# Experts' rows added into X in DRAM by the scatter's own transfers, and a feed-forward opened in another order

## The chip, the cores and the metric

One core of a Trainium2 chip runs the whole kernel in one launch. The metric is the device time of an execution in microseconds (us); less is better. The kernel before was run three times.

## What is computed

Two layers over 16 sequences of 128 tokens of 256 numbers (2048 tokens), each a gated cross-attention and a gated feed-forward, added to x. Cut to what the change touches:

```python
x = x + tanh(g_xattn[0]) * mlstm(layernorm(x), ctx, ctx, ...)
x = x + tanh(g_ffn[0])   * ffn0(layernorm(x), ...)     # 8 experts, 2 per token, and 2 shared ones
x = x + tanh(g_xattn[1]) * attention(layernorm(x), ctx, mask, ...)   # 16 heads of 16
x = x + tanh(g_ffn[1])   * ffn1(layernorm(x), ...)     # 16 experts in 4 groups, 4 per token, and a shared one

# ffn0
logits = xf @ router_w.T + expert_bias
rw, sel = top_k(logits, 2); rw = softmax(rw)
combine = einsum('tk,tke->te', rw, one_hot(sel, 8))
out = sum over e of combine[:, e] * (silu(xf @ w1[e].T) * (xf @ w3[e].T)) @ w2[e].T
out = out + the same for the two shared experts, without weights
```

## The kernel before

X, the 2048 rows of x, stays on the chip as 128 partitions x 16 sequences x 256, in four chunks of four sequences (`CH` = 4, `NCH` = 4). The work goes through five stages in one program; each engine has its own list of instructions, written out by hand, and semaphores join them.

The first attention (`front`, `cell`) and the shared experts of the first feed-forward (`shared_feed_forward`) come first. While the shared experts run, each token's normalised row is scattered twice into `xg_dram`, sorted by expert, with its destination and its weight behind it. `routed_tiles` then takes 39 tiles (`NT`) of 128 such rows. For a tile i, SyncE loads its rows into `t_x` (L2121), TensorE turns them (L2144), makes gate (L2153 to L2155) and up (L2162), turns the hidden rows (L2169) and makes the down product (L2180); ScalarE and VectorE copy between them; VectorE multiplies by the row's weight (L2252); and GpSimd scatters the 128 result rows into `y_dram` in DRAM (`send`, L2134). Each token has two places there, one for each of its experts, and the blank rows of partly filled tiles have places of their own. `y`, `dest` and `t_x` have two buffers each. With the last `t_x` load SyncE issues the seven loads of `later` (L2124): the weights, context and masks of the second attention.

`attention_feed_forward` holds the second attention and the second feed-forward. It opens with the projections of keys and values of chunks 0 and 1, which need no x. When all scatters have landed, SyncE loads both places of every token into `picked` (L728), 8 transfers for 4 chunks. VectorE adds chunk 0 to X (`add_first`, L1247), GpSimd adds chunks 1 to 3 (L787) in 12 instructions. Then come, chunk by chunk, the layer norm: `statistics2` (VectorE, L1256, L1259), `deviation2` (ScalarE's square root, L1075), `scale2` (VectorE), `normalise2` (both); TensorE turns the rows (`project` of kind "x", L846), and makes the queries from them (L858). A softmax step s (16 of them, one per sequence) is: scores (TensorE, L873), `soft` (VectorE, twice, L1286 and L1289), `centre` (GpSimd, L814), `exps` (ScalarE, L1092 and L1096), turning (TensorE, L885), `keep_turned` (ScalarE for three quarters, VectorE for the last, L1295), `values` (TensorE, L897), and the output added to X by GpSimd (L822).

The feed-forward runs in steps u, 12 (`U`) per chunk: `gate_up(u)` and `down(u)` (L981) on TensorE, `silu` (L1136) and `keep_hhi` (L1147) on ScalarE, `hidden` on VectorE. Beside the steps of a chunk the next chunk is prepared; a function `step(u, c)` says at which step which piece comes: statistics, deviation, normalise, turning (`turn_xn`, L920), the copies of the turned rows (`keep_hi`, `keep_lo`), router (L931), the route steps on VectorE (`route_logits` to `route_weights`), `turn_comb` and `keep_comb`, after which SyncE stores the combine weights and loads them as `cb`. The third block of weights is split by ScalarE in two halves (`last_block_hi`, L1142) and by VectorE in three thirds.

The order of the first steps of VectorE before, word for word:

```python
for n in range(2):
    keep((0, "v", n))
add_first()
statistics2(0)
scale2(0)
normalise2(0)
keep((0, "x", 1))
for n in range(2):
    keep((1, "v", n))
statistics2(1)
scale2(1)
normalise2(1)
```

## Time and profile before

| | us |
|---|---|
| median of 3 runs | 883.3 |
| lowest, highest | 883.18, 890.21 |
| the profiled execution | 890.36 |
| its span | 888.2 |
| expert tiles, first to last scatter's issue | 276.9 to 483.4 |
| loads of `picked` start | 485.77 |
| TensorE busy, whole span | 783.9 |

The span is what the profiler saw of the instructions; the execution's own time is a little longer. The three runs lie on two levels, and the profiled execution on the upper. Times of instructions are counted from the span's start. A row of the view in order of time gives start, length, engine, line, operation, output<-input and number of instructions, and in brackets the engine's idle time before it and what ended it. PE is TensorE's products, PEld its weight loads, DVE VectorE, ACT ScalarE, POOL GpSimd, SPq SyncE's transfers.

### The profile page before, as it was taken

What the parts mean: (1) busy time and instruction counts of PE and PEld (TensorE: products, weight loads), DVE (VectorE), ACT (ScalarE), POOL (GpSimd) and SP (SyncE); (2) the same over time, 40 slices, a digit from 0 to 9 for tenths busy, and PEclk for the clock granted to TensorE, in tenths of its full rate; (3) what the DMA queues carried; (4) which work ended last, traced back from release to release, by engine and by line L of the source; (5) the groups of instructions that cost most, each with busy time, mean ns of one, the idle gap of its engine ahead of it and who ended that gap; (6) DMA issues with size and microseconds to landing.
All of it is one profiled execution on the core that took longest, in us unless ns stands there. A gap on an engine that the chain in (4) does not pass through costs nothing.

```text
span 888.2 us, 14817 instructions
## 1 busy us (share of the span) xinstructions
PE 783.9 (88%) x5188; PEld 609.4 (69%) x5188; DVE 512.2 (58%) x1188; ACT 395.6 (45%) x806; POOL 220.4 (25%) x220
## 2 busy tenths in 40 slices
PE   4556399999999999999999778996788999999997
PEld 3345277788887777777776445664567888888886
DVE  4478865565454444333342678879755675756644
ACT  5468545234342222222222378787645335253322
POOL 0179110026602111111113448675210000000000
PEclk9788889999999999999999879999888999999999
DMA  8357651013241111111133800202004005050130
GB/s 296 122 187 288 229 203 59 1 54 120 90 154 42 49 49 49 52 50 48 49 90 114 290 0 13 75 11 73 1 1 97 1 1 120 1 120 1 37 84 25
DMA packets 33591, 74.32 MB, mean 84 GB/s; under 512 B 4400, under 2 KB 20400, under 8 KB 31760
## 3 DMA queue, kind: packets, MB, share of 16 engines
q1 hardware_dynamic: 30112, 64.03, 23.0%
q0 software_dynamic: 3408, 9.34, 2.9%
q8 instruction: 44, 0.72, 0.3%
q14 instruction: 27, 0.22, 0.1%
HBM read 61.73 MB, written 16.78 MB: 88 GB/s over the span
## 4 chain that ended last, share of the span: by engine, by line
PE 61%; DVE 11%; ACT 5%; issue 4%; DVEq 3%; DMA 1%; POOL 1%; POOLq 1%; SPq 0%; ACTq 0%
PE t_y_ps L2180 8%; PE t_up L2162 8%; PE f_y L1743 4%; PE a_turned L981 4%; PE a_score L959 3%; PE a_score L961 3%; PE a_score L960 3%; PE a_turned L885 2%; PE t_gate L2153 2%; PE t_gate L2154 2%; PE t_gate L2155 2%; PE t_h_turned L2169 2%; PE a_proj L858 2%; PE a_out_ps L981 1%; PE f_gate L1724 1%
## 5 line engine op out<-in xcount | busy, mean ns | idle before, releaser
L2212 ACT CAST t_xT_hi<-t_x_turned 128x256 fp32r<-128x256 f32 x39 | 14.5, 372 | 150.3 <-PE t_x_turned L2144 150.3
L2134 POOL DMA_INDIRECT outputs<-t_y,t_dest x39 | 37.4, 959 | 177.4 <-DVEq L2253 174.8
L2180 PEld LDWEIGHTS t_y_ps<-W,t_hidT 128*128 128x128 f32 x312 | 59.2, 190 | 25.2 <-issue 19.2
L2180 PE MATMUL t_y_ps<-W,t_hidT 128*128 x312 | 73.8, 379 | 0.8 <-ACT t_hidT L2222 0.8
L2162 PE MATMUL t_up<-W,t_xT 128*128 x156 | 73.4, 593 | 0.0
L1147 ACT CAST a_hhi<-a_hid 128x512 fp32r<-128x512 f32 x48 | 29.8, 620 | 76.9 <-DVEq L1441 76.9
L1136 ACT ACTIVATE a_act_g<-a_score 128x512 f32<-128x512 f32 x48 | 28.7, 597 | 59.0 <-PE a_score L961 58.8
L1443 DVE TENSOR_TENSOR a_hlo<-a_hid,a_hhi 128x512 fp32r<-128x512 f32 x48 | 33.2, 693 | 35.1 <-ACT a_hhi L1147 35.1
L2241 DVE TENSOR_TENSOR t_hid<-t_act_g,t_up 128x512 f32<-128x512 f32 x39 | 26.8, 688 | 38.5 <-ACT t_act_g L2217 34.2
L1096 ACT ACTIVATE a_pr<-a_sc,a_nmx 128x128 f32<-128x128 f32 x128 | 40.8, 391 | 13.4 <-DVE a_nmx L1289 13.4
L814 POOL TENSOR_TENSOR a_sc<-a_sc,a_nmx 128x512 f32<-128x512 f32 x32 | 33.2, 1039 | 51.8 <-DVE a_nmx L1289 51.8
L2232 DVE COPY t_xT<-t_x_turned 128x256 f32<-128x256 f32 x39 | 16.6, 425 | 47.0 <-ACT t_xT_hi L2212 46.9
L885 PE MATMUL a_turned<-cst,a_pr 128*128 128x128 f32 x256 | 41.0, 297 | 1.9 <-ACT a_prT L1102 1.9
L1286 DVE TENSOR_TENSOR a_sc<-a_score,a_pen 128x1024 f32<-128x1024 f32 x32 | 38.9, 1217 | 5.8 <-PE a_score L873 4.5
L443 ACT ACTIVATE W<-W,AT 128x128 f32<-128x128 f32 x128 | 38.2, 390 | 7.1 <-POOL W L359 7.1
L2252 DVE TENSOR_SCALAR t_y<-t_y_ps,t_dest 128x256 f32<-128x256 f32 x39 | 18.9, 483 | 38.8 <-PE t_y_ps L2180 38.8
L1289 DVE TENSOR_REDUCE a_nmx<-a_sc 128x8 f32<-128x1024 f32 x32 | 39.0, 1220 | 2.9
L897 PE MATMUL a_out_ps<-a_prT,a_v 128*32 128x128 f32 x512 | 25.8, 295 | 16.5 <-issue 10.7
L2162 PEld LDWEIGHTS t_up<-W,t_xT 128*128 128x128 f32 x156 | 26.6, 190 | 18.6 <-issue 18.6
L2153 PE MATMUL t_gate<-whi,t_xT_hi 128*128 x78 | 37.9, 486 | 1.3 <-DVE t_xT_lo L2233 1.3
L885 PEld LDWEIGHTS a_turned<-cst,a_pr 128*128 128x128 f32 x256 | 30.0, 151 | 11.7 <-issue 8.7
L1651 POOL DMA_INDIRECT slot_tokens<-W,slots x32 | 34.0, 1064 | 15.1 <-issue 15.1
...
## 6 DMA issues: line engine op xcount, KB each, us to landing
...
t_x<-slot_tokens SPq DMA_DIRECT2D x39, 129.0 KB, 2.0
...
```

Of the source, the lines that this page charges most:

```text
L443: last = act.activation(dmat[i % 2][:, q, k, r], expo[i % 2][:, q, k, r], ACT.Exp, bias=AT[:, at:at + 1], scale=-1.0)
L885: last = pe.transpose(turned[n % 2][:, i * 128:(i + 1) * 128], pr[s % 2][:, g, i], cst[:, C_ID:C_ID + 128])
L981: last = pe.matmul(y_bank[use % 3][:, (j % 2) * D:(j % 2 + 1) * D], h[q][:, j * 128:(j + 1) * 128], w_[:, down_cols(ht)], start=first, sto ...
L1096: last = act.activation(pr[s % 2][:, g, i], sc[s % 2][:, g, i], ACT.Exp, bias=nmx[s % 2][:, g, i:i + 1])
L1286: dve.tensor_tensor(part, score[:, half * 1024:(half + 1) * 1024].rearrange("p (h t) -> p h t", h=8), pen[c % 2][:, j:j + 1].broadcast_to( ...
L1289: dve.tensor_reduce(nmx[s % 2][:, 2 * half:2 * half + 2].rearrange("p r i -> p (r i)"), part, AX.X, ALU.max, negate=True).then_inc(max_rea ...
L1651: pool.indirect_dma_start(xg_dram, bass.IndirectOffsetOnAxis(ap=slots[:, k, s:s + 1], axis=0), XN[:, s, :], None).then_inc(done, 16)
L1743: last = pe.matmul(y_bank[use % 3][:, (j % 2) * D:(j % 2 + 1) * D], h_[q][:, j * 128:(j + 1) * 128], w_[:, down_cols(ht)], start=first, st ...
L2134: pool.indirect_dma_start(y_dram, bass.IndirectOffsetOnAxis(ap=dest[p][:, 0:1].bitcast(U32), axis=0), y[p][:], None).then_inc(y_stored[p], 16)
L2153: pe.matmul(gate[p][:], xT_hi[p][:, k], W_hi[:, ds(e, 1), cols], start=(k == 0), stop=False)
L2162: last = pe.matmul(up[p][:], xT[p][:, k], W[:, ds(e, 1), at:at + HID], start=(k == 0), stop=(k == KT - 1))
L2180: last = pe.matmul(y_ps[p][:, 0:D], hidT[p][:, h], W[:, ds(e, 1), at:at + D], start=(h == 0), stop=(h == HT - 1))
```

## The change

It has four parts.

1. The sum in DRAM. `y_dram` goes; `sum_dram` has one row per token and 128 rows that are written by blank rows only (set to zeros early, so that they hold numbers). SyncE stores X into it, chunk by chunk, as soon as a chunk is complete: chunks 0 and 1 behind the load of expert 7's weights, chunk 2 between the loads of expert 1's weights, chunk 3 behind the second `t_x` load. GpSimd's scatters have a `compute_op` that adds to the row at the destination; the first waits for all stores, and each waits for the one before. At the attention's opening X is loaded from there in four transfers. `picked`, `add_first` and GpSimd's adds go.
2. The order at the attention's opening, on VectorE and ScalarE: statistics and scales of chunks 2 and 3 ahead of the first softmax; chunk 1's statistics ahead of the copy of chunk 0's second turned half; one small activation loads the square root's table while ScalarE waits for the scatters.
3. The end of the attention: VectorE's copy of the last turned probabilities comes ahead of `route_logits` and of `route_second`, which goes behind the first hidden product. `last_block_hi(0)` moves from step 2 to step 1.
4. The steady feed-forward: for chunks 2 and 3 turning and all that follows it come one step later; statistics, deviation and normalising stay.

```diff
@@ cell, SyncE @@
             sp.dma_start(xg_dram.rearrange("(p i) d -> p (i d)", p=128),
                          blank_rows.rearrange("(p i) d -> p (i d)", p=128)).then_inc(slots_blank, 16)
+            sp.dma_start(sum_dram[T:T + 128, :], blank_rows[0:128, 0:D]).then_inc(sums_blank, 16)
@@ attention_feed_forward @@
-        by_dve = [(0, "v", 0), (0, "v", 1), (0, "x", 1), (1, "v", 0), (1, "v", 1)]
+        by_dve = [(0, "v", 0), (0, "v", 1), (1, "v", 0), (0, "x", 1), (1, "v", 1)]
...
         def step(u, c):
-            return u - ((c - 1) * U + (1 if c == 1 else 0))
+            k = u - ((c - 1) * U + (1 if c == 1 else 0))
+            return k if c == 1 or k < 2 else (k - 1 if k > 2 else None)
+
+        def normalised(u, c):
+            return u - ((c - 1) * U + (1 if c == 1 else 0)) == 2
@@ SyncE @@
-            rows = y_dram[0:2 * T, :].rearrange("(k s p) d -> p k s d", k=2, s=B)
             for c in range(NCH):
                 part = slice(c * CH, (c + 1) * CH)
-                for k in range(2):
-                    sp.dma_start(picked[:, k, part, :], rows[:, k, part, :]).then_inc(picked_loaded[c], 16)
+                sp.dma_start(X[:, part, :], sums[:, part, :]).then_inc(x_loaded[c], 16)
@@ GpSimd @@
-            pool.wait_ge(first_added, 1)
-            for c in range(1, NCH):
-                pool.wait_ge(picked_loaded[c], 32)
-                for half in range(2):
-                    at = slice(c * CH + 2 * half, c * CH + 2 * half + 2)
-                    for k in range(2):
-                        last = pool.tensor_tensor(X[:, at, :], X[:, at, :], picked[:, k, at, :], ALU.add)
...
@@ ScalarE @@
+            act.activation(largest[:, 0, 0:1], cst[:, C_EPS:C_EPS + 1], ACT.Sqrt)
+
             for p in range(2):
                 act.wait_ge(y_stored[p], 16 * ((NT + 1 - p) // 2))
-            for n in range(2):
-                keep((1, "k", n))
+            keep((1, "k", 0))
             deviation2(0)
             normalise2(0)
+            keep((1, "k", 1))
             keep((0, "x", 0))
             deviation2(1)
-            for n in range(2):
-                keep((0, "q", n))
             normalise2(1)
+            keep((0, "q", 0))
+            deviation2(2)
+            keep((0, "q", 1))
+            deviation2(3)
...
-                if 2 <= u < 4:
-                    last_block_hi(u - 2)
+                if u in (1, 3):
+                    last_block_hi(u // 2)
@@ VectorE @@
             def statistics2(c):
-                wait(dve, picked_added, c)
+                dve.wait_ge(x_loaded[c], 16)
...
-            add_first()
             statistics2(0)
             scale2(0)
             normalise2(0)
+            keep((1, "v", 0))
+            statistics2(1)
             keep((0, "x", 1))
-            for n in range(2):
-                keep((1, "v", n))
-            statistics2(1)
+            keep((1, "v", 1))
             scale2(1)
             normalise2(1)
+            for c in (2, 3):
+                statistics2(c)
+            for c in (2, 3):
+                scale2(c)
...
                 keep(early)
+                if s == B:
+                    route_groups(0)
+                if past:
+                    keep_turned(s - 1, 3)
                 if s == B - 1:
                     route_logits(0)
-                elif s == B:
-                    route_groups(0)
-                    route_second(0)
-                if past:
-                    keep_turned(s - 1, 3)
...
                 elif s == B:
                     hidden(0)
+                    route_second(0)
                     route_pick(0)
@@ shared_feed_forward, SyncE @@
+            def store(c):
+                sp.wait_ge(y_free, 2 * c + 2)
+                sp.dma_start(sums[:, c * CH:(c + 1) * CH, :], X[:, c * CH:(c + 1) * CH, :]).then_inc(x_stored[c], 16)
...
@@ routed_tiles, SyncE and GpSimd @@
                 sp.dma_start(x[p][:], xg_dram[ds(i * 128, 128), :]).then_inc(x_loaded[p], 16)
+                if i == 1:
+                    sp.wait_ge(y_free, 2 * NCH)
+                    sp.dma_start(sums[:, (NCH - 1) * CH:, :], X[:, (NCH - 1) * CH:, :]).then_inc(x_stored[NCH - 1], 16)
...
             def send(i, p, nth):
                 pool.wait_ge(y_ready, i + 1)
+                wait(pool, y_stored[1 - p], 16 * ((i + 1) // 2))
                 pool.sem_inc(sent, 1)
-                pool.indirect_dma_start(y_dram, bass.IndirectOffsetOnAxis(ap=dest[p][:, 0:1].bitcast(U32), axis=0), y[p][:],
-                                        None).then_inc(y_stored[p], 16)
+                pool.indirect_dma_start(sum_dram, bass.IndirectOffsetOnAxis(ap=dest[p][:, 0:1].bitcast(U32), axis=0), y[p][:],
+                                        None, compute_op=ALU.add).then_inc(y_stored[p], 16)
+            pool.wait_ge(sums_blank, 16)
+            for c in range(NCH):
+                pool.wait_ge(x_stored[c], 16)
```

How the instructions stand in a row, at the three places that matter. SyncE's list at the start of the tiles, before (W: expert weights, t_x: a tile's rows):

```order
L1633 DMA W<-in_w_dram 128x2560
L1635 DMA W<-in_w_dram 128x512 [waits f_hlo_ready]
L2116 UNCONDITIONAL_BRANCH
L2121 DMA t_x<-slot_tokens 128x258 [waits f_h_used]
L2121 DMA t_x<-slot_tokens 128x258
L2121 DMA t_x<-slot_tokens 128x258 [waits t_dest_ready,t_xt_ready] x37
```

and after the change:

```order
L1619 DMA W<-in_w_dram 128x2560
L1603 DMA sums<-X 128x4x256 [waits f_y_free]
L1622 DMA W<-in_w_dram 128x512 [waits f_hlo_ready]
L2105 UNCONDITIONAL_BRANCH
L2110 DMA t_x<-slot_tokens 128x258 [waits f_h_used]
L2110 DMA t_x<-slot_tokens 128x258
L2113 DMA sums<-X 128x4x256 [waits f_y_free]
L2110 DMA t_x<-slot_tokens 128x258 [waits t_dest_ready,t_xt_ready] x37
```

The first of the stores shown is chunk 2's, ahead of the last part of expert 1's weights; the second is chunk 3's, and it stands between the second and the third `t_x` load and waits for the last sum of X.

VectorE at the attention's opening before, behind chunk 0's normalised rows and up to the first softmax (a_XNT: turned rows, a_v: values, a_stats: statistics, a_pr: normalised rows, a_sc: scores with the mask):

```order
L1226 COPY a_XNT<-a_turned 128x2x256 [waits a_proj_ready]
L1238 SCALAR_TENSOR_TENSOR a_v<-a_score,g_tanh,a_bvt 128x16x16 [waits a_proj_ready]
L1238 SCALAR_TENSOR_TENSOR a_v<-a_score,g_tanh,a_bvt 128x16x16
L1238 SCALAR_TENSOR_TENSOR a_v<-a_score,g_tanh,a_bvt 128x16x16 [waits a_proj_ready]
L1238 SCALAR_TENSOR_TENSOR a_v<-a_score,g_tanh,a_bvt 128x16x16
L1256 BN_STATS a_stats<-X 128x6 [waits a_picked_added]
L1256 BN_STATS a_stats<-X 128x6 x3
L1259 BN_AGGR a_mean_var<-a_stats 128x2 x4
L1265 RECIPROCAL a_rstd<-a_std 128x4 [waits a_std2_ready]
L1267 SCALAR_TENSOR_TENSOR a_shift<-a_mean_var,a_rstd 128x4
L1275 TENSOR_SCALAR a_pr<-X,a_mean_var,a_rstd 128x256 x2
L1286 TENSOR_TENSOR a_sc<-a_score,a_pen 128x1024 [waits a_pen_ready,a_score_ready]
```

and after:

```order
L1230 SCALAR_TENSOR_TENSOR a_v<-a_score,g_tanh,a_bvt 128x16x16 [waits a_proj_ready]
L1230 SCALAR_TENSOR_TENSOR a_v<-a_score,g_tanh,a_bvt 128x16x16
L1239 BN_STATS a_stats<-X 128x6 [waits a_x_loaded1]
L1239 BN_STATS a_stats<-X 128x6 x3
L1242 BN_AGGR a_mean_var<-a_stats 128x2 x4
L1218 COPY a_XNT<-a_turned 128x2x256 [waits a_proj_ready]
L1230 SCALAR_TENSOR_TENSOR a_v<-a_score,g_tanh,a_bvt 128x16x16 [waits a_proj_ready]
L1230 SCALAR_TENSOR_TENSOR a_v<-a_score,g_tanh,a_bvt 128x16x16
L1248 RECIPROCAL a_rstd<-a_std 128x4 [waits a_std2_ready]
L1250 SCALAR_TENSOR_TENSOR a_shift<-a_mean_var,a_rstd 128x4
L1258 TENSOR_SCALAR a_pr<-X,a_mean_var,a_rstd 128x256 x2
L1239 BN_STATS a_stats<-X 128x6 [waits a_x_loaded2]
```

Chunk 1's statistics and a copy of values moved ahead of the copy into `a_XNT`, and where the softmax stood the statistics of chunk 2 begin; those of chunk 3 and both scales follow before the softmax.

ScalarE there before, from chunk 0's square roots on (a_std: square roots, a_kbd: keys, a_qT: queries):

```order
L1075 ACT_TABLE_LOAD
L1075 ACTIVATE a_std<-a_mean_var,cst 128x4 [waits a_var2_ready]
L1084 ACTIVATE a_pr<-X,a_shift,a_rstd 128x256 [waits a_shift2_ready]
L1084 ACTIVATE a_pr<-X,a_shift,a_rstd 128x256
L1059 COPY a_XNT<-a_turned 128x2x256 [waits a_proj_ready]
L1075 ACTIVATE a_std<-a_mean_var,cst 128x4 [waits a_var2_ready]
L1063 ACTIVATE a_qT<-a_out_ps,a_bq 128x512 [waits a_proj_ready]
L1063 ACTIVATE a_qT<-a_proj,a_bq 128x512 [waits a_proj_ready]
L1084 ACTIVATE a_pr<-X,a_shift,a_rstd 128x256 [waits a_shift2_ready]
L1084 ACTIVATE a_pr<-X,a_shift,a_rstd 128x256
L1059 COPY a_XNT<-a_turned 128x2x256 [waits a_proj_ready] x2
```

and after:

```order
L1066 ACTIVATE a_std<-a_mean_var,cst 128x4 [waits a_var2_ready]
L1075 ACTIVATE a_pr<-X,a_shift,a_rstd 128x256 [waits a_shift2_ready]
L1075 ACTIVATE a_pr<-X,a_shift,a_rstd 128x256
L1059 ACTIVATE a_kbd<-a_score,a_bkm,cst 128x512 [waits a_proj_ready]
L1059 ACTIVATE a_kbd<-a_score,a_bkm,cst 128x512
L1050 COPY a_XNT<-a_turned 128x2x256 [waits a_proj_ready]
L1066 ACTIVATE a_std<-a_mean_var,cst 128x4 [waits a_var2_ready]
L1075 ACTIVATE a_pr<-X,a_shift,a_rstd 128x256 [waits a_shift2_ready]
L1075 ACTIVATE a_pr<-X,a_shift,a_rstd 128x256
L1054 ACTIVATE a_qT<-a_out_ps,a_bq 128x512 [waits a_proj_ready]
L1066 ACTIVATE a_std<-a_mean_var,cst 128x4 [waits a_var2_ready]
L1054 ACTIVATE a_qT<-a_proj,a_bq 128x512 [waits a_proj_ready]
```

The table load is gone from here (it stands ahead of the wait for the scatters now), a copy of keys went behind the first normalised rows, chunk 1's rows went ahead of the queries, and the root of chunk 2 stands between the two query copies.

## Rows read from the trace of the kernel before

**Rows 1.** Busy time by stretch (us; PE, PEld, DVE, ACT, POOL, PEclk, DMA, GB/s).

```profile
300.00:350.00 50.00, 50.00 (x218) 36.34 (x217) 19.88 (x56) 13.68 (x29) 8.63 (x9) 1.00 0.17 50
500.00:550.00 50.00, 38.19 (x301) 22.28 (x301) 39.02 (x71) 34.70 (x79) 33.67 (x35) 0.85 0.14 54
650.00:700.00 50.00, 44.12 (x269) 35.98 (x269) 31.31 (x94) 25.26 (x42) 2.50 (x3) 0.90 0.20 44
```

**Rows 2.** Instructions in order of time, the last tiles, POOL and DVE.

```profile
452.62 0.96 POOL L2134 DMA_INDIRECT outputs<-t_y,t_dest  x1 [4.53 <-DVEq L2253]
458.11 0.96 POOL L2134 DMA_INDIRECT outputs<-t_y,t_dest  x1 [4.54 <-DVEq L2253]
...
471.69 0.17 DVE L2245 COPY t_dest<-t_next_dest 128x2 int32<-128x2 int32 x1 [3.42 <-DMA outputs<-t_y,t_dest]
...
479.86 0.96 POOL L2134 DMA_INDIRECT outputs<-t_y,t_dest  x1 [4.27 <-DVEq L2253]
```

**Rows 3.** The tensor of results: all its scatters, then the one at 463.60 alone.

```profile
L2134 POOL DMA_INDIRECT outputs<-t_y,t_dest x39: 954/958/967, 276.9 to 483.4; - x39
...
DMA to landing us min/median/max: 2.4/2.4/10.8
...
L2134 POOL DMA_INDIRECT outputs<-t_y,t_dest x1: 958/958/958, 463.6 to 463.6; - x1
...
DMA to landing us min/median/max: 8.1/8.1/8.1
```

**Rows 4.** The page's transfers: KB each, median us from issue to landing.

```profile
t_x<-slot_tokens SPq DMA_DIRECT2D x39, 129.0 KB, 2.0
```

**Rows 5.** Instructions in order of time, the opening of the second attention.

```profile
491.06 2.52 DVE L1247 TENSOR_TENSOR X<-X,a_picked 128x1024 f32<-128x1024 f32 x2 [1.54 <-DMA a_picked<-outputs]
...
491.88 3.62 PE L851 MATMUL a_score<-a_w,a_keyT 128*128 128x256 f32 x16
...
493.68 1.40 DVE L1256 BATCH_NORM_STATS2 a_stats<-X 128x6 f32<-128x256 f32 x4
...
506.25 9.24 POOL L787 TENSOR_TENSOR X<-X,a_picked 128x512 f32<-128x512 f32 x7 [0.15 <-issue]
...
506.82 0.30 ACT L1075 ACTIVATE a_std<-a_mean_var,cst 128x4 f32<-128x4 f32 x1 [7.16 <-DVEq L1260]
...
510.21 1.21 DVE L1286 TENSOR_TENSOR a_sc<-a_score,a_pen 128x1024 f32<-128x1024 f32 x1
...
515.10 1.39 DVE L1256 BATCH_NORM_STATS2 a_stats<-X 128x6 f32<-128x256 f32 x4
...
519.11 1.23 DVE L1286 TENSOR_TENSOR a_sc<-a_score,a_pen 128x1024 f32<-128x1024 f32 x1 [0.19 <-issue]
...
522.39 1.28 ACT L1075 ACT_TABLE_LOAD   x1
...
530.47 1.22 DVE L1286 TENSOR_TENSOR a_sc<-a_score,a_pen 128x1024 f32<-128x1024 f32 x1 [1.94 <-PE a_score L873]
...
537.04 1.21 DVE L1286 TENSOR_TENSOR a_sc<-a_score,a_pen 128x1024 f32<-128x1024 f32 x1
...
544.04 1.22 DVE L1286 TENSOR_TENSOR a_sc<-a_score,a_pen 128x1024 f32<-128x1024 f32 x1
```

**Rows 6.** The output's last store, of 512 KB, alone on the queues.

```profile
L764 SPq DMA_DIRECT2D out_dram<-X x1: 377/377/377, 884.8 to 884.8; - x1
...
DMA to landing us min/median/max: 2.9/2.9/2.9
```

**Rows 7.** Instructions in order of time, the start of the tiles.

```profile
266.24 1.65 DVE L2067 SCALAR_TENSOR_TENSOR X<-f_y,g_tanh,X 128x256 f32<-128x256 f32 x4
...
271.22 0.38 PE L2144 MATMUL t_x_turned<-cst,t_x 128*128 128x128 f32 x2
```

**Rows 8.** Instructions in order of time, the opening of the second feed-forward.

```profile
661.20 0.43 PE L897 MATMUL a_out_ps<-a_prT,a_v 128*32 128x128 f32 x8 [1.63 <-DVE a_prT L1295]
...
674.76 1.48 ACT L1142 CAST a_block2hi<-a_raw 128x1536 fp32r<-128x1536 f32 x1
...
681.23 0.38 PE L981 MATMUL a_turned<-a_block0hi,a_hhi 128*128 128x256 f32 x1 [1.87 <-ACT a_hhi L1147]
```

**Rows 9.** Who waited for whom, 684 to 888 us: total, times, longest.

```profile
PE a_proj L920 <- DVE a_xn L1328: 1.8, 3, 0.7
```

65 lines of the change are left out of this document (25 added, 40 removed).

## The prediction

> **What bounds the kernel now.** I read the busy times by stretch first, then who waited for whom, and only then single instructions in order of time. In the expert tiles (300 to 350 us) TensorE has no gap at all, at the full granted clock, while VectorE, ScalarE and GpSimd have room. In 500 to 550 us it is busy for 38.19 of 50 us at a mean granted clock of 0.85: that is the opening of the second attention. In 650 to 700 us it is busy for 44.12, the opening of the second feed-forward [rows 1]. What the change does to work beside the tiles is worth nothing by itself; its worth has to be found at the two openings.
>
> The last expert's scatter is issued at 483.36 (483.4 in the view of its tile) and lands 2.4 us later, at 485.8 [rows 3], and then the eight loads of `picked` start. From there on [rows 5]: VectorE adds chunk 0 at 491.06 (2.52 us for both adds), the statistics begin at 493.68, GpSimd adds chunks 1 to 3 until 506.25 + 9.24 = 515.49. ScalarE's root for chunk 1, which needs those sums, begins at 506.82 and stands in its queue ahead of the copies of the queries, without which there are no scores; the first softmax starts at 510.21. After it VectorE has the statistics of chunks 2 and 3 (from 515.10) ahead of the next softmax at 519.11, and ScalarE loads another table at 522.39. The third softmax begins at 530.47; then a step takes 7.00 us (537.04 to 544.04).
>
> **Part 1: the sums made by the transfers.** What goes: 4 of 8 loads of 512 KB, VectorE's two adds and GpSimd's twelve. What comes: each scatter adds to rows in DRAM, and each waits until the one before has landed. How long such a scatter takes stands in no row. From below it can be as short as a plain one, 2.4 us to landing, of which 0.96 is GpSimd writing the descriptors [rows 3]. From above I take a plain one and a read of its own, as long as the load of the same rows into `t_x`, 2.0 us [rows 4]: 4.4; further out lies the 8.1 us that a plain one took from 463.60 on, beside the seven loads for the attention [rows 3]. I take the middle of the first two, 3.4. The Trainium skill (DMA: Bandwidth & Descriptors, Rules for kernel authors) says that an accumulating transfer reads its destination and writes it later, so that the next one has to wait for its semaphore. The change does that; the trace of before has no accumulating transfer to compare. The same page (Latency and other measured facts) gives about 0.8 us as the least round trip to DRAM; a plain 2.4 and that would make an estimate of 3.2.
>
> A tile takes 5.49 us (scatters at 452.62 and 458.11 [rows 2]), so at 3.4 us each scatter has landed before the next result is ready, and the added wait costs nothing. Nothing else stands behind it on GpSimd until the tiles end, and VectorE waits only for the scatter two tiles back. Two places have no such room. Beside the seven loads a scatter took 8.1 us and VectorE stood 3.42 us for it, at 471.69 [rows 2]; a longer one there holds TensorE up by at most what it adds, 1.0; I take 0.5, between 0 and 2.0. At the end scatter 37 is issued at 479.86 [rows 2] and lands at 483.3, and 38, issued at 483.4 as before, lands at 486.8 instead of 485.8: 1.0 (0 if it is a plain one; 2.9 at 4.4 us each, since 38 is then also issued 0.9 later).
>
> The rows of X have to be in DRAM first. The stores of chunks 0 to 2 fall beside the shared experts, and ahead of nothing on SyncE that is soon wanted. The store of chunk 3 stands ahead of the third `t_x` load, whose rows are turned at 271.22 now. That load would come after the last sum of X (266.24 + 1.65 = 267.89 [rows 7]), behind 512 KB in the same queue. A store of this size took 2.9 us alone [rows 6]; some 1.5 of that I take as data. So the load lands near 268.4 + 2.0 + 1.5 = 271.9 against 271.22: 0.7, between 0 and 3.
>
> **Part 2: the attention's opening.** I go on from the new landing at 486.8. X's chunk 0 is one transfer of 512 KB instead of two: between 2.9 us (the store alone) and the 5.3 us of the first pair (485.8 to 491.06), I take 3.8: 490.6. Statistics (1.40 and their grouping), the root (0.30, its table loaded before), scale and the normalised rows take some 4.1: 494.7. TensorE still projects values of chunk 1 until 491.88 + 3.62 = 495.5 and turns the rows by some 496.7. VectorE's copy of them now stands behind a copy of values and chunk 1's statistics: 498.0. The queries are as much work as those values, 3.6: 501.7. ScalarE copies the first half by 501.1, then waits until 502.0 for chunk 2's statistics on VectorE, takes the root and copies the second by 503.1. The first scores run to 504.3, chunk 3's root and the two scales end at 505.1, and the first softmax starts at 505.1: 5.1 earlier than 510.21, with the later scatter already in it.
>
> From the first softmax to the third it is 530.47 - 510.21 = 20.26 us now, against 14.0 for two steady steps. What goes of the difference: VectorE's statistics, 4.0 (515.10 to 519.11); two table loads of ScalarE (1.28 each, one at 522.39); and GpSimd's adds until 515.49, which hold up its own part of the first softmax [rows 5]. They overlap, and the floor is 14.0. I take 14.9, which gives 5.4 more. From the third softmax on both run at 7.00 a step and nothing is given back. Sum of this part: -10.5. I count nothing for the granted clock, though shorter gaps may raise its 0.85 here.
>
> **Part 3: the feed-forward's opening.** TensorE waits 1.63 us at 661.20 for VectorE's copy of the last turned probabilities, which stands behind two route steps [rows 8]. Now it stands behind one, and TensorE gets 1.1 back. But VectorE idles those 1.1 until the turning is done, with all its route steps still to do, so its product for step 1 comes 1 us later and TensorE loses the gain there. The first half of the third weight block (1.48 us of ScalarE at 674.76) moves a step forward, where ScalarE has idle time; it stood ahead of the activation whose product TensorE waits for, 1.87 us at 681.23 [rows 8]. With VectorE's 1.0 against it 0.4 is left: -0.4.
>
> Later turning: for chunks 2 and 3 the rows are turned one step after they are normalised, where TensorE now waits 0.6 each (1.8 in three waits [rows 9]; that of chunk 1 stays): -1.2. All route steps of the two chunks come one step later too; their combine weights are then made at the same distance from their use as chunk 1's now, and the waits from 684 us on show none for `cb`.
>
> **The sum:** -10.5 + 0.5 + 0.7 - 0.4 - 1.2 = -10.9. The profiled execution took 890.36 us (span 888.2, the rest lies around it), so 879.5 for its like. The median of the runs is 883.3, 7.1 below the profiled one: two runs are near 883 and one is at 890.21. I put the difference on the median: 872.4, given as 872.5.
>
> **Rivals.** A, the opening keeps much of its length: the chain through statistics, turning and queries is serial, the statistics of chunks 2 and 3 now stand ahead of the first softmax, and the two first steps still carry extra copies and projections, so VectorE and ScalarE become the bound. For it speaks that ScalarE's second query copy waits for chunk 2's statistics; against it, that VectorE idles there anyway. Then only the 5.1 to the first softmax come, less 0.5 and 0.7 and with part 3: -5.5, 878. B, the transfers become the bound of the tiles: an adding scatter with twice the 0.96 us of descriptors, a read of 2.0, the 1.4 that is left of a plain one and 0.7 for the add takes 6.0, and with half a us from landing to the next issue it paces a tile at 6.5 instead of 5.49. Over 38 tiles +38, less 10 at the openings: 911. It decides from about 5.0 us per scatter on; for it speaks only that a plain one took 8.1 in company. C, more comes: TensorE keeps its clock through the opening (the mean is 0.85 now) and the first two steps come near their floor: -16, 867. D, the last scatters pile up behind the seven loads: two of 8 us in a row delay VectorE and then the end of the tiles by 4 to 5: 877.
>
> **How the numbers follow.** Forecast 0.55, A 0.17, B 0.10, C 0.09, D 0.09. Faster by over 1% is below 874.5, and about 1% is what a measurement of this kernel can tell from no change. The forecast's own range is 868 to 877, of which some three quarters lie below (0.42); with C and a part of A and D (0.05) that is 0.56. Slower is B and a little for what I overlooked: 0.11. The rest, 0.33, is within 1%. The range takes in C below, and A, D and a median that falls on the upper of the two levels above: 866 to 884; B stays outside.
>
> **What would show it.** In the profile after: scatters of 3 to 4 us to landing and tiles still 5.49 apart; the third turning of `t_x` at most 3 us later; the first softmax 18 us after the last landing and the third 15 later; one table load fewer on either side of it; TensorE's wait at the last turned probabilities smaller by 1.1, and two of three waits for `a_xn` gone. A tile pace above 5.5, a scatter above 5 us, or a first softmax that is not earlier would make the forecast wrong.

## The result, and the profile after

| | before | changed |
|---|---|---|
| median, on the first chip | 885.12 us (9 runs, 881.27 to 890.21) | 879.03 us (9 runs, 875.92 to 881.86) |
| ratio | | 0.9929, 95% interval 0.9901 to 0.9956 |
| the profiled execution | 890.36 | 876.65 |
| its span, mean granted clock | 888.2, 0.952 | 874.8, 0.966 |

The change takes 6.1 us off the medians (0.7%), where 10.9 were forecast. The two profiled executions differ by 13.7, more than twice that, so the first thing to learn is which part of that difference belongs to the change and which to the draw of two executions. Two executions of the kernel before beside e5 to e8 took 1950 and 2992 us (the others 887 to 898) and are in none of the ratios there.

The busy times of the three stretches after:

```profile
300.00:350.00 50.00, 50.00 (x218) 36.37 (x218) 20.09 (x56) 13.65 (x29) 14.57 (x10) 1.00 0.30 49
500.00:550.00 50.00, 42.00 (x365) 24.54 (x365) 41.19 (x77) 38.40 (x90) 24.73 (x28) 0.93 0.15 59
650.00:700.00 50.00, 47.03 (x268) 40.58 (x267) 33.96 (x102) 22.85 (x33) 0.73 (x1) 0.97 0.21 44
```

The tiles have no gap on TensorE, as before. GpSimd is busy for 14.57 us there in place of 8.63, and the DMA share is 0.30 in place of 0.17: that is the adding, since in e10, the same kernel without it, they are 8.62 and 0.16. At both openings TensorE has smaller gaps and a higher clock than in [rows 1].

The page's row of the adding scatter (instructions, busy time and mean ns of one), and its tile's view of the 35 from 300 us on (busy ns of one, then us from issue to landing):

```profile
L2127 POOL DMA_INDIRECT sums<-t_y,t_dest x39 | 60.8, 1559 | 160.3 <-DVEq L2249 142.2
...
L2127 POOL DMA_INDIRECT sums<-t_y,t_dest x35: 1556/1557/1558, 299.3 to 488.4; - x35
...
DMA to landing us min/median/max: 3.7/3.9/9.6
```

It lands after 3.9 us in place of 2.4 and takes GpSimd 1.56 us in place of 0.96 [rows 3]. The forecast took 3.4 to landing. (Both views of the tile count the loads from it too: the 10.8 us in [rows 3] is a load of `picked`, and the longest landing of a scatter there is 8.1.)

The last tiles in order of time, GpSimd's and VectorE's rows, which answer to [rows 2]:

```profile
458.61 1.56 POOL L2127 DMA_INDIRECT sums<-t_y,t_dest  x1 [3.94 <-DVEq L2249]
464.10 1.56 POOL L2127 DMA_INDIRECT sums<-t_y,t_dest  x1 [3.94 <-DVEq L2249]
474.50 1.56 POOL L2127 DMA_INDIRECT sums<-t_y,t_dest  x1 [8.85 <-DMA sums<-t_y,t_dest]
479.01 1.56 POOL L2127 DMA_INDIRECT sums<-t_y,t_dest  x1 [2.95 <-DMA sums<-t_y,t_dest]
483.93 1.56 POOL L2127 DMA_INDIRECT sums<-t_y,t_dest  x1 [3.36 <-issue]
488.39 1.56 POOL L2127 DMA_INDIRECT sums<-t_y,t_dest  x1 [2.90 <-DMA sums<-t_y,t_dest]
...
473.77 0.17 DVE L2241 COPY t_dest<-t_next_dest 128x2 int32<-128x2 int32 x1 [5.01 <-DMA sums<-t_y,t_dest]
...
478.28 0.17 DVE L2241 COPY t_dest<-t_next_dest 128x2 int32<-128x2 int32 x1 [2.39 <-DMA sums<-t_y,t_dest]
...
482.88 0.17 DVE L2241 COPY t_dest<-t_next_dest 128x2 int32<-128x2 int32 x1 [1.84 <-DMA sums<-t_y,t_dest]
```

The pace of 5.49 us holds up to the scatter at 464.10. The next is released by a landing (`<-DMA sums`), not by VectorE, 10.4 us later, and then they follow at 4.5 to 4.9. VectorE, which may not overwrite `dest` before its scatter has landed, waits 5.01, 2.39 and 1.84 us where it waited 3.42 once.

The start of the tiles, as in [rows 7]:

```profile
267.18 0.38 PE L2140 MATMUL t_x_turned<-cst,t_x 128*128 128x128 f32 x2
271.65 0.44 PE L2140 MATMUL t_x_turned<-cst,t_x 128*128 128x128 f32 x2 [0.98 <-DMA t_x<-slot_tokens]
```

A wait of 0.98 us for the third load of `t_x`, where TensorE had none. In e5 and e13, two more executions of the same kernel, it is 0.78 and none.

The attention's opening after, which answers to [rows 5]:

```profile
495.92 1.41 DVE L1239 BATCH_NORM_STATS2 a_stats<-X 128x6 f32<-128x256 f32 x4 [4.39 <-DMA X<-sums]
...
504.26 1.40 DVE L1239 BATCH_NORM_STATS2 a_stats<-X 128x6 f32<-128x256 f32 x4
...
511.02 1.23 DVE L1269 TENSOR_TENSOR a_sc<-a_score,a_pen 128x1024 f32<-128x1024 f32 x1 [0.67 <-PE a_score L864]
...
515.96 1.22 DVE L1269 TENSOR_TENSOR a_sc<-a_score,a_pen 128x1024 f32<-128x1024 f32 x1
...
523.55 1.22 DVE L1269 TENSOR_TENSOR a_sc<-a_score,a_pen 128x1024 f32<-128x1024 f32 x1 [0.64 <-PE a_score L864]
...
488.66 1.28 ACT L1143 ACT_TABLE_LOAD   x1
...
492.18 2.03 SPq L729 DMA_DIRECT2D X<-sums  x4
```

X is asked for at 492.18 and its first chunk has landed at 495.92. VectorE then has the statistics of all four chunks ahead of the first softmax at 511.02. From there to the third (523.55) it takes 12.53 us in place of 20.26 (17.1 and 18.9 in e8 and e7, which have the opening of the kernel before), and ScalarE's table load for the roots stands at 488.66, where ScalarE had nothing to do.

Who waited for whom on TensorE at the end of the attention and in the feed-forward (total, times, longest):

```profile
PE a_turned L972 <- ACT a_hhi L1138: 3.5, 5, 1.7
PE a_proj L930 <- DVE a_comb L1394: 1.3, 1, 1.3
PE a_out_ps L972 <- ACT a_hhi L1138: 0.5, 1, 0.5
PE a_out_ps L888 <- DVE a_prT L1278: 0.4, 1, 0.4
```

The wait for the turned probabilities is 0.4 in place of 1.63, that for `a_xn` is gone, and one for the combine weights (1.3) is new.

### The profile page after: what moved, and what is told of

It reads as the page before. It is cut to its first block, busy times and chain, and to the rows that moved or that the text cites. A ratio compares the mean times of both kernels' runs of the same rounds, so it can differ in the third digit from the quotient of the medians.

```text
span 874.8 us, 14796 instructions
## 1 busy us (share of the span) xinstructions
PE 773.7 (88%) x5188; PEld 601.4 (69%) x5188; DVE 507.3 (58%) x1186; ACT 392.6 (45%) x805; POOL 228.9 (26%) x208
## 4 chain that ended last, share of the span: by engine, by line
PE 54%; DVE 15%; ACT 8%; issue 4%; DMA 4%; DVEq 4%; SPq 0%; ACTq 0%; POOLq 0%
PE t_y_ps L2176 7%; PE t_up L2158 7%; PE f_y L1730 4%; DMA sums<-t_y,t_dest 3%; PE a_turned L972 2%; PE a_turned L876 2%; ACT a_hhi L1138 2%; PE a_score L950 2%; PE a_score L952 2%; PE a_score L951 2%; PE a_proj L849 2%; DVE a_hlo L1426 2%; PE t_gate L2150 2%; PE t_gate L2151 2%; PE t_gate L2149 2%
## 5 line engine op out<-in xcount | busy, mean ns | idle before, releaser
L2127 POOL DMA_INDIRECT sums<-t_y,t_dest x39 | 60.8, 1559 | 160.3 <-DVEq L2249 142.2
L1087 ACT ACTIVATE a_pr<-a_sc,a_nmx 128x128 f32<-128x128 f32 x128 | 40.8, 391 | 13.2 <-DVE a_nmx L1272 12.5
L2248 DVE TENSOR_SCALAR t_y<-t_y_ps,t_dest 128x256 f32<-128x256 f32 x39 | 18.9, 484 | 37.1 <-PE t_y_ps L2176 37.1
L2158 PEld LDWEIGHTS t_up<-W,t_xT 128*128 128x128 f32 x156 | 26.6, 191 | 18.6 <-issue 18.6
L876 PE MATMUL a_turned<-cst,a_pr 128*128 128x128 f32 x256 | 38.2, 282 | 0.5 <-ACT a_prT L1093 0.5
L888 PE MATMUL a_out_ps<-a_prT,a_v 128*32 128x128 f32 x512 | 24.7, 286 | 15.2 <-issue 10.9
L1418 DVE TENSOR_TENSOR a_hid<-a_score,a_cb 128x512 f32<-128x512 f32 x32 | 22.1, 691 | 21.8 <-PE a_score L952 19.1
```

The source lines that it names most:

```text
L876: last = pe.transpose(turned[n % 2][:, i * 128:(i + 1) * 128], pr[s % 2][:, g, i], cst[:, C_ID:C_ID + 128])
L1087: last = act.activation(pr[s % 2][:, g, i], sc[s % 2][:, g, i], ACT.Exp, bias=nmx[s % 2][:, g, i:i + 1])
L2127: pool.indirect_dma_start(sum_dram, bass.IndirectOffsetOnAxis(ap=dest[p][:, 0:1].bitcast(U32), axis=0), y[p][:], None, compute_op=ALU.add) ...
L2158: last = pe.matmul(up[p][:], xT[p][:, k], W[:, ds(e, 1), at:at + HID], start=(k == 0), stop=(k == KT - 1))
```

## The measure for the experiments

The start of the tiles (the first turning of `t_x`) falls at 263.96 us in this profile and at 273.11 in another one of the same kernel. Most stretches behind it are steady to some tenths; F and D are not, as said below. So the experiments are read by seven stretches, each between two rows: A from the first turning of `t_x` to the first scatter; B from there to the last scatter; C to the first statistics of X; D to ScalarE's first exponents (L1087); E to its exponents of the third softmax; F to its last exponents; G to the last write of X. All are in us, in the traces of the kernel before, of that kernel with one wait added (e8) and with seven loads spread (e7), neither of which changed its time, and of the changed kernel in three executions.

| | before | e8 | e7 | changed | e5 | e13 |
|---|---|---|---|---|---|---|
| A | 12.17 | 12.17 | 12.16 | 13.49 | 13.28 | 12.57 |
| B | 206.51 | 206.55 | 206.52 | 210.94 | 211.11 | 210.17 |
| C | 10.32 | 10.59 | 10.53 | 7.53 | 7.67 | 7.53 |
| D | 19.76 | 19.12 | 19.61 | 18.06 | 17.15 | 17.18 |
| E | 20.74 | 19.33 | 18.56 | 13.61 | 13.61 | 13.61 |
| F | 117.41 | 116.70 | 114.74 | 113.58 | 117.81 | 113.85 |
| G | 231.57 | 229.77 | 229.63 | 228.57 | 229.00 | 230.01 |
| A to G | 618.48 | 614.23 | 611.75 | 605.78 | 609.63 | 604.92 |

The changed kernel averages 606.8 and the other three 614.8. In F the last step takes 5.0 us in the changed kernel's first trace and in e13, and 9.3 in e5, which is the same kernel. In e5 TensorE has no gap but half the clock from 642.4 to 651.7 us (granted 0.50; 1.00 in the same step of e13), as the stretch that holds this step shows (TensorE's busy time first, granted clock third from the end):

```profile
640.00:650.00 10.00, 10.00 (x80) 8.25 (x81) 5.28 (x5) 4.49 (x11) 3.04 (x4) 0.58 0.00 1
```

The kernel before was profiled in such an execution (9.6 us, clock 0.57 in the same stretch); e8 and e7 took 6.5. That is one reason why the two first profiles overstate the change.

## Experiments

Each ratio is to runs of the kernel before on the same chip, whose median there was 890.4 to 891.4 us; a median alone is not compared with one of the first chip.

**e1 and e12, the seven loads spread.** In SyncE's load function:

```diff
-                if isinstance(i, int) and i == NT - 1:
-                    for dst, src, loaded in later:
-                        sp.dma_start(dst, src).then_inc(loaded, 16)
+                for dst, src, loaded in later[i - (NT - 8):i - (NT - 8) + 1] if i >= NT - 8 else []:
+                    sp.dma_start(dst, src).then_inc(loaded, 16)
```

> The changed kernel with the seven loads for the attention (w, bqk, bv, keyT, pen) issued one behind each of the x loads of tiles 31 to 37, instead of all seven behind the load of tile 38. Theory (the last scatters pile up behind the seven loads, each adding scatter waiting for the one before it): the scatter of tile 34 lands about 4 us after its issue in place of 9.6, the VectorE waits of 5.01, 2.39 and 1.84 us in the last five tiles go or fall below 1 us, the first load of X is issued 4 to 6 us earlier than at 492.18 us, and the whole takes 4 to 5 us less than the changed kernel, about 874.5 us in the median. Rival 1 (the tiles are late by the adding scatters' own landing of 3.9 us and their serial wait, the loads are incidental): the first load of X moves by less than 1 us and the time stays at 879. Rival 2 (the load is 3.8 MB in any case and slows scatters wherever it stands): several tiles wait 1 to 2 us each, and the gain is below 2 us.

Measured: 879.57 us, ratio 0.9863 (0.9832 to 0.9893). GpSimd's rows of the last tiles:

```profile
475.25 1.56 POOL L2126 DMA_INDIRECT sums<-t_y,t_dest  x1 [3.94 <-DVEq L2248]
480.74 1.56 POOL L2126 DMA_INDIRECT sums<-t_y,t_dest  x1 [3.94 <-DVEq L2248]
486.35 1.56 POOL L2126 DMA_INDIRECT sums<-t_y,t_dest  x1 [4.04 <-issue]
490.76 1.56 POOL L2126 DMA_INDIRECT sums<-t_y,t_dest  x1 [2.86 <-DMA sums<-t_y,t_dest]
```

The pile-up is gone: B is 207.65, 3.3 less than in the changed kernel's trace, and rival 1 falls. What stays over 206.51 is 1.1, in the last two intervals (5.61 and 4.41 in place of 5.22 and 3.50); the last scatter waits for the one before. (The seven loads are 2.4 MB, by the sizes of the issues in the profile, not 3.8.) D was 15.56 too, 2.5 less. The two executions' rows show why (changed kernel first, then e1): the queries ran at half clock in the one (granted 0.50 from 502.7 to 506.5 us) and at full clock in the other. The next four products took 2.71 and 1.88.

```profile
502.74 3.75 PE L849 MATMUL a_out_ps<-a_XNT,a_w 128*128 128x512 f32 x4 [1.82 <-DVE a_XNT L1218]
```

```profile
505.16 1.96 PE L849 MATMUL a_out_ps<-a_XNT,a_w 128*128 128x512 f32 x4 [1.82 <-DVE a_XNT L1218]
```

To see whether this is worth its 4 to 5 us in the median, it was timed again beside the changed kernel itself.

> The changed kernel with the seven loads spread, once more, beside the changed kernel itself on the same chip. The stretches of the traces say 3.3 us from the first scatter to the last and 1.5 to 2.5 us in the queries' clock; one kernel's attention ends in 4.9 or 9.4 us for its last step from run to run, so single profiles and medians of few runs hide it. Theory (the pile-up is worth 4 to 5 us): the median is 3.5 to 5.5 us below that of the changed kernel in this call. Rival (what the last scatters give is taken back behind them, as the run with both repairs had it with 0.9901): less than 2 us below.

> The changed kernel as it is, beside the run before this one: 210.6 to 211.1 us from the first scatter to the last, a ratio to the kernel before of 0.991 to 0.994, and 3.5 to 5.5 us more than the kernel with the loads spread by the theory, under 2 us more by the rival.

Measured: 883.21 and 882.64 us, ratios 0.9906 (0.9877 to 0.9934) and 0.9921 (0.9890 to 0.9952). B was 207.80 against 210.17, so the tiles were again 2.4 shorter, but D was 17.18 in both: the full clock of the queries in e1 was a draw. The median with the loads spread is 0.6 us above that of the changed kernel beside it, not 4 to 5 below, and this theory of the size falls, though e1's ratio alone had agreed with it; by this pair it is under 2 as the rival had it. The rival's reason is not borne out either: from the first scatter to the last write of X e12 took 590.13 and e13 592.35, so nothing behind the tiles took the gain back. The starts of the tiles, 275.55 and 269.37, differ by more than what is looked for.

**e2, the store of chunk 3 behind the third load of `t_x`:**

```diff
-                if i == 1:
+                if i == 2:
```

> The changed kernel with the store of X's fourth chunk behind the load of x for tile 2 instead of ahead of it. Theory (the store on SP's queue holds up x(2)): TensorE's wait of 0.98 us for t_x at 271.65 us goes, the tiles start 0.5 to 1.1 us earlier, the whole is about 1 us shorter, which 5 rounds hardly tell from nothing; GpSimd's first scatter is not later, since tile 0's rows are ready only after the store has landed. Rival (hidden anyway: TensorE then waits for the copies of x_turned or for a later load): the milestone of tile 38 moves by less than 0.2 us. Rival 2: the store lands later and the first adding scatter waits for it, the first tiles lengthen by up to 1 us.

Measured: 885.15 us, 0.9908 (0.9881 to 0.9935). A was 12.28, that is 0.3 to 1.2 less than the changed kernel's three, and the wait of TensorE is gone; but e13 had no such wait either, so only the 12.28, met again in e11, speaks for the edit. The store does hold the load up; the price is small, and below what the median can tell.

**e3, the opening's order put back** (X still comes whole from DRAM):

```diff
+            keep((0, "x", 1))
-            keep((1, "v", 0))
-            statistics2(1)
-            keep((0, "x", 1))
-            keep((1, "v", 1))
+            for n in range(2):
+                keep((1, "v", n))
+            statistics2(1)
             scale2(1)
             normalise2(1)
-            for c in (2, 3):
-                statistics2(c)
...
-            act.activation(largest[:, 0, 0:1], cst[:, C_EPS:C_EPS + 1], ACT.Sqrt)
```

> The changed kernel with the order of the attention's opening put back as it was in the kernel before (statistics of chunks 2 and 3 and the deviations in step 0 and 1, keeps of keys and values ahead of the normalising, no early Sqrt), while X still comes whole from DRAM. Theory (the order carries the gain, as the forecast had it): from the first softmax to the third it takes again about 20 us in place of 12.5, or at least 17, and the whole is 5 to 8 us longer than the changed kernel. Rival (the gain comes from taking away the additions on GpSimd and VectorE and the second half of the loads alone, so that chunks 2 and 3 are there when step 0 wants them; the order is worth little): the third softmax moves by less than 2 us against the landing of X. Between them: 2 to 5 us, shared.

Measured: 888.36 us (12 runs), 0.9956 (0.9934 to 0.9979). VectorE's rows:

```profile
499.03 1.41 DVE L1238 BATCH_NORM_STATS2 a_stats<-X 128x6 f32<-128x256 f32 x4 [4.05 <-DMA X<-sums]
...
510.92 1.23 DVE L1268 TENSOR_TENSOR a_sc<-a_score,a_pen 128x1024 f32<-128x1024 f32 x1 [1.35 <-PE a_score L864]
...
515.82 1.40 DVE L1238 BATCH_NORM_STATS2 a_stats<-X 128x6 f32<-128x256 f32 x4
...
527.83 1.23 DVE L1268 TENSOR_TENSOR a_sc<-a_score,a_pen 128x1024 f32<-128x1024 f32 x1 [0.30 <-PE a_score L864]
```

With the old order the first softmax stands 11.89 us behind the first statistics, in place of 15.10, and the third 16.91 behind the first, in place of 12.53. The order moves work from between the softmaxes to ahead of them; at the third it is worth 1.2 us by these rows (28.80 against 27.63), 1.0 to 1.9 by D + E against the three executions. Without the order, D + E is 32.65, against 38.17 in e7, 38.45 in e8 and 40.50 in the kernel before: these 5.5 to 7.9 us come from the additions and the second half of the loads that are gone, which no run separates. So the rival holds in the traces. The median, 0.9956 against 0.9915 to 0.9929, says some 3 us for the order, with intervals that overlap; its profile had the last attention step in 9.6 us at a clock of 0.67 in 640 to 650, and whether the old order meets the half clock there more often stays open.

**e4, the router's steps and the halves of the third block put back:**

```diff
-                if s == B:
-                    route_groups(0)
-                if past:
-                    keep_turned(s - 1, 3)
                 if s == B - 1:
                     route_logits(0)
+                elif s == B:
+                    route_groups(0)
+                    route_second(0)
+                if past:
+                    keep_turned(s - 1, 3)
                 keep(late)
...
-                if u in (1, 3):
-                    last_block_hi(u // 2)
+                if 2 <= u < 4:
+                    last_block_hi(u - 2)
```

> The changed kernel with the router's steps (route_groups, route_second ahead of the copies again) and last_block_hi at u = 2 and 3 put back as in the kernel before. Theory (the forecast's -0.4 for this part): the waits of TensorE on a_prT (0.43 us) grows to about 1.6 us, that on a_comb (1.30 us) goes, hidden(0) to hidden(1) is shorter by about 1 us, and the whole stays within 1 us. Rival 1 (this part keeps the granted clock up: the kernel before ran at 0.57 in 640 to 650 us and at 0.66 in 680 to 690): the row at the end of the attention shows a stretch at half clock again and the whole is 3 to 4 us longer. Rival 2 (it costs: the a_comb wait is new and holds the second unit): the whole is 1 to 2 us shorter.

Measured: 882.64 us, 0.9915 (0.9885 to 0.9944). TensorE's waits:

```profile
PE a_out_ps L888 <- DVE a_prT L1278: 3.4, 2, 1.8
PE a_proj L911 <- DVE a_xn L1311: 0.8, 1, 0.8
```

The wait for `a_prT` is back, the one for `a_comb` gone. From the first silu to the last write of X it takes 222.58 us against 222.07, 222.50 and 222.08 of the changed kernel: 0.1 to 0.5, as forecast, and below what the medians can tell. Rival 1 does not hold in this trace, whose last attention step took 5.0 us again.

Its tiles, which the edit does not touch, show something else. GpSimd's rows:

```profile
468.02 1.56 POOL L2127 DMA_INDIRECT sums<-t_y,t_dest  x1 [3.93 <-DVEq L2249]
476.86 1.56 POOL L2127 DMA_INDIRECT sums<-t_y,t_dest  x1 [7.29 <-DMA sums<-t_y,t_dest]
481.19 1.56 POOL L2127 DMA_INDIRECT sums<-t_y,t_dest  x1 [2.78 <-DMA sums<-t_y,t_dest]
485.96 1.56 POOL L2127 DMA_INDIRECT sums<-t_y,t_dest  x1 [3.21 <-issue]
490.41 1.56 POOL L2127 DMA_INDIRECT sums<-t_y,t_dest  x1 [2.90 <-DMA sums<-t_y,t_dest]
```

The late scatter landed after 8.1 us and the next came 8.84 behind it, where the changed kernel's three executions have 10.0 to 11.0; B is 209.04, so 2.5 is lost and not 3.7 to 4.6.

**e5, the changed kernel again, and e6, the early stores moved.** In four profiles of kernels that differ from the changed one only behind this place (e1 to e4), TensorE stood 3 to 4 us in 200 to 220 us.

> The changed kernel as it is, beside the next runs on the same chip. In the first profile of it the scatters of slot tokens' stretch (200 to 220 us) shows TensorE busy for all 20 us; in four kernels that differ only behind it TensorE was busy 16.1 to 17.0 us there and stood 3.9 to 4.4 us on nothing that the profile names, while the load of W and the two stores of X filled the DMA engines from 198 to 208 us. Theory (the stores lengthen that stretch, and an engine's instructions, which come over the same DMA engines, are late in some executions): the stall shows here too or not by chance, and the median is 4 to 8 us below that of the kernel before rather than the 13 that the parts sum to. Rival (it was that chip): here as in the first profile no stall, and the ratio is below 0.99.

```diff
-            store(0)
-            store(1)
             for p in range(2):
                 sp.wait_ge(scattered[p], 16 * B // 2)
-                sp.wait_ge(scattered2[p], 16 * B // 2)
+            store(0)
+            sp.wait_ge(scattered2[0], 16 * B // 2)
+            store(1)
+            sp.wait_ge(scattered2[1], 16 * B // 2)
```

> The changed kernel with the stores of X's first two chunks taken from behind the 1.5 MB load of W: the first goes behind the first sixteen scatters of slot tokens, the second behind the next eight (about 216 and 228 us in place of 194 and 201). Theory (they crowd the DMA engines at 198 to 208 us and make an engine's instructions late): TensorE is busy all 20 us of 200:220, the first row of the tiles starts 4 us earlier than where the stall shows, and the median is 2 to 4 us below the changed kernel's. Rival 1 (the stall has another cause, the chip's or the order's): same TensorE share, same median within 1 us. Rival 2 (the stores now meet the token scatters and delay their end, then the load of W, by 1 us each): up to 2 us longer.

Measured: e5 884.63 us, 0.9915 (0.9883 to 0.9948); e6 884.48 us, 0.9913 (0.9885 to 0.9941). TensorE's busy time in that stretch was 14.01 in e5, 16.86 in e6, and in e8, which is the kernel before with one wait and no stores at all:

```profile
200.00:220.00 20.00, 15.45 (x80) 13.37 (x79) 9.58 (x14) 6.75 (x10) 13.53 (x16) 0.91 0.34 126
```

The stall is not made by the stores, and the theory falls. It is in every trace but those of the two first profiles, of both kernels alike, so I take it to stand on both sides of the ratios; what it is stays open.

**e7, the kernel before with the seven loads spread** (the edit of e1).

> The kernel before with the seven loads for the attention spread over the x loads of tiles 31 to 37. Control of the spreading: VectorE's wait of 3.42 us in the last tiles goes; from the first scatter to the last it took 206.5 us, and I expect 205 to 206.5, since the waits there were partly hidden; the whole within 2 us. Theory (only adding scatters, each waiting for the one before, make a queue of the seven loads costly: 3.3 us in the changed kernel against under 1.5 here). Rival (the loads cost the same before the change, so the pile-up was no part of what the change did): 3 us or more shorter here too.

Measured: 891.59 us, 1.0011 (0.9984 to 1.0039); B is 206.52. The loads cost the kernel before nothing.

**e8, the kernel before with the serial wait alone:**

```diff
                 pool.wait_ge(y_ready, i + 1)
+                wait(pool, y_stored[1 - p], 16 * ((i + 1) // 2))
```

> The kernel before with one added wait: each plain scatter of a tile's rows waits on GpSimd until the one before it has landed. It prices the serial order without the adding. Theory (in the steady tiles the wait is hidden, 5.5 us between scatters against a landing of 2.4): 5.49 us between scatters as before; at the end the scatter behind the one that lands after 8 to 10.8 us is issued 2 to 4 us later, and from the first scatter to the last it takes 1 to 3 us more than 206.5, against the 4.4 more of the changed kernel. Rival 1 (the wait costs all of it): 4 us or more. Rival 2 (nothing: the last scatters come from VectorE's pace): below 0.5 us.

Measured: 892.02 us, 1.0018 (0.9988 to 1.0048); B is 206.55, so rival 2 holds. The rows:

```profile
469.73 0.96 POOL L2135 DMA_INDIRECT outputs<-t_y,t_dest  x1 [4.53 <-DVEq L2254]
478.56 0.96 POOL L2135 DMA_INDIRECT outputs<-t_y,t_dest  x1 [7.87 <-DMA outputs<-t_y,t_dest]
482.01 0.96 POOL L2135 DMA_INDIRECT outputs<-t_y,t_dest  x1 [2.49 <-DMA outputs<-t_y,t_dest]
485.99 0.96 POOL L2135 DMA_INDIRECT outputs<-t_y,t_dest  x1 [3.02 <-DVEq L2254]
489.50 0.96 POOL L2135 DMA_INDIRECT outputs<-t_y,t_dest  x1 [2.54 <-issue]
```

One scatter is 3.3 us late (8.83 after the one before, in place of 5.49; it landed after 8.1 us), and the next follow at 3.45 to 3.98, until at the end nothing is lost. The serial wait is free where what is queued behind it can catch up.

**e9, the later turning undone:**

```diff
-            k = u - ((c - 1) * U + (1 if c == 1 else 0))
-            return k if c == 1 or k < 2 else (k - 1 if k > 2 else None)
+            return u - ((c - 1) * U + (1 if c == 1 else 0))
```

> The changed kernel with the feed-forward's later rows turned, stored and normalised at the steps of the kernel before. The changed kernel takes 222.1 us from the first silu to the last write of X, the kernel before 223.1 to 225.1. Theory (the later turning takes away the waits of TensorE on a_xn, 1.8 us before and none after): a_xn is waited for again, 1.5 to 2 us in three waits, the stretch takes 223 to 224 us, and the whole is 1 to 2 us longer than the changed kernel. Rival (the waits were hidden or only move): the stretch stays within 0.3 us of 222.1.

Measured: 884.80 us (11 runs), 0.9937 (0.9916 to 0.9958). TensorE's wait came back, but the stretch from the first silu took 222.31 us, inside the 222.07 to 222.50 of the changed kernel:

```profile
PE a_proj L910 <- DVE a_xn L1310: 1.9, 3, 0.8
```

The rival holds: the waits for `a_xn` were covered, and the term of 1.2 us was at most 0.2 (222.31 against 222.07 and 222.08 in the two executions with the short last step). The ratio is 0.0008 to 0.0022 above those of the changed kernel, less than the intervals can tell.

**e10, the adding left out:**

```diff
-                                        None, compute_op=ALU.add).then_inc(y_stored[p], 16)
+                                        None).then_inc(y_stored[p], 16)
```

> The changed kernel with the scatters' adding left out: each tile's rows overwrite those of the tokens in the same buffer, with the same waits, so the output misses the sums and only its time counts. Before: 206.5 us from the first scatter to the last. Changed: 210.6 to 211.1. The kernel before with the serial wait alone: 206.55, since scatters that are queued follow at 3.5 to 4.0 us and catch up. Theory (it is the adding scatter's slower landing, 3.9 us for 2.4, and GpSimd's 1.56 us for 0.96, that keeps the last scatters at 4.5 us and from catching up): 206.5 to 207.5 us, scatters 35 to 38 at 3.5 to 4.0 us, and the whole 3 to 4 us shorter. Rival (the 128 rows past the tokens, a smaller buffer, or the rows of T that many tiles share): 210 us or more, the adding is free.

Measured: 880.69 us, 0.9878 (0.9845 to 0.9911); B is 206.42 and C 6.15. The last scatters:

```profile
471.36 0.96 POOL L2127 DMA_INDIRECT sums<-t_y,t_dest  x1 [4.53 <-DVEq L2249]
480.16 0.96 POOL L2127 DMA_INDIRECT sums<-t_y,t_dest  x1 [7.84 <-DMA sums<-t_y,t_dest]
484.12 0.96 POOL L2127 DMA_INDIRECT sums<-t_y,t_dest  x1 [3.00 <-DMA sums<-t_y,t_dest]
487.95 0.96 POOL L2127 DMA_INDIRECT sums<-t_y,t_dest  x1 [2.87 <-issue]
491.11 0.96 POOL L2127 DMA_INDIRECT sums<-t_y,t_dest  x1 [2.21 <-DMA sums<-t_y,t_dest]
```

Same buffer, same waits, same seven loads, and B is that of the kernel before. So the adding itself makes the 3.7 to 4.6 us in B and the 1.4 in C (7.53 against 6.15, the slower last landing). The ratio is 0.0037 to 0.0051 below those of the changed kernel (3 to 5 us), with intervals that overlap. This kernel leaves the sums out, so it shows a price and is no version to use. Against e8 and e4, whose late scatter set the queue back as far (8.83 and 8.84), the price in B has two parts: about 2.5 us because adding scatters catch up less, and the rest, in the changed kernel's three executions, because the late one itself came 10.0 to 11.0 behind.

**e11, both repairs:** the edits of e1 and e2.

> The changed kernel with both repairs: the attention's seven loads one behind each x load of tiles 31 to 37, and the store of X's fourth chunk behind the load of tile 2. Theory (the parts add): 12.3 us from the first turning to the first scatter (changed: 13.3), 207.6 us from the first scatter to the last (changed: 210.9), queries at full clock in the opening (1.96 us in place of 3.75), and the whole 5.5 to 6.5 us shorter than the changed kernel, a ratio of 0.984 to 0.987 to the kernel before. Rival (the earlier tiles only meet another wait): the ratio is that of the spreading alone, 0.986, or above 0.99.

Measured: 881.71 us, 0.9901 (0.9871 to 0.9931). A is 12.28 and B 207.76 as expected, D 17.11; but F was 117.85, with its last step in 9.4 us. The gain in the tiles is there and the median did not show it. The three ratios with the loads spread (0.9863, 0.9906, 0.9901) average 0.9890 and the three of the changed kernel (0.9929, 0.9915, 0.9921) 0.9922: in the right direction by about 3 us, but the intervals overlap, so a version that beats both kernels is not shown.

## Why the prediction was wrong

The direction, the bound and most mechanisms held; the size did not, and 879.0 is 6.5 us above the forecast. It is nearest to rival A's 878, but by luck: A's mechanism would have left the stretch from the first softmax to the third as it was, and that became shorter than forecast. Point by point:

- **Adding scatter in steady tiles: right.** 3.9 us to landing (forecast 3.4), below the 5.49 of a tile, and the pace stays 5.49. Rival B is out. The Trainium skill (DMA: Bandwidth & Descriptors, Latency and other measured facts) had led to an estimate of 3.2 from its 0.8 us, which it gives as the least round trip to DRAM. The trace has 3.9, so the estimate was too low; no run here shows a round trip by itself.
- **The step that failed: "a longer one there holds TensorE up by at most what it adds, 1.0; I take 0.5".** With the 1.0 of the last landing, the forecast had 1.5 for the end of the tiles. Measured: 3.7 to 4.6 in B and 1.4 in the last landing, so 5.1 to 6.0. (e4, with the same tiles, has 2.5 in B.) I added one scatter's lateness once. What the runs showed in its place: the late scatter beside the seven loads sets a queue back by 3.3 to 5.5 us, and the queue drains only as far as its own time per scatter lies below the tile's pace. Plain scatters drain it at 3.2 to 4.0 us (e8, e10: B 206.4 to 206.6), adding ones only at 4.2 to 4.9, and after the late one only three are left. The late one is longer as well: 9.2 to 10.2 us to landing in three traces and 8.1 in e4, against 8.0 to 8.1 for a plain one. Neither the serial wait (e8) nor the loads (e7) cost the kernel before anything; adding and loads together do (e1, e10). It is rival D, "two of 8 us in a row delay VectorE and then the end of the tiles by 4 to 5: 877", which I gave 0.09, though its one premise was wrong: one late scatter is enough.
- **The store ahead of the third load: right.** +0.4 to +1.3 in A (forecast 0.7); without it (e2, e11) +0.1.
- **From the last landing to the first softmax: right in size.** From 492.18 to 511.02 are 18.8 us, forecast 18.3. It is 18.0 in e5 and e13. Part of why it is no shorter is that VectorE has all statistics ahead, as rival A feared: with the old order (e3) it is 15.6, and the time is lost again behind the first softmax.
- **From the first softmax to the third: shorter than forecast.** 12.5 us where I took 14.9 and a "floor" of 14.0. Two early steps have less output work than two steady ones (by the kernel's text; no run tests it), so two steady steps are no floor. By ScalarE's rows (E) the kernel before took 20.7 when profiled, 19.3 in e8 and 18.6 in e7, the changed one 13.6, so this is worth 5.0 to 7.1 (forecast 5.4). I had put it to the order as much as to the additions; over the whole opening (D and E) e3 gives the order 1 to 2 us.
- **The feed-forward: smaller than forecast.** The route order 0.1 to 0.5 (forecast 0.4), the later turning 0.2 at most (forecast 1.2). From the first silu to the last write of X e7 and e8 took 223.1 and 223.3 us and the changed kernel 222.1 to 222.5, so both together gave 0.6 to 1.2. I had read an engine's wait as a gain without asking what would be late next.
- **The base.** I took the terms from one execution of 890.36 us and subtracted their sum from a median. That execution had F and G of 348.98 us against 346.47 in e8 and 344.37 in e7, partly at half clock. And the median of three runs, 883.3, became 885.12 with nine, which do not lie on two levels: 1.8 of the 6.5 us are the base alone. The change gave 8.0 us between the averages of the three columns and the three, and 6 to 8 by the ratios.

With the end of the tiles at +5.1 to +6.0 in place of +1.5 and the later turning at 0, my own sum comes to -10.9 + 1.2 and another 3.6 to 4.5, that is -5.2 to -6.1; the medians and ratios say -6.1 to -7.6.
